# Masked attention layer on one core: the start laid anew, later tokens turned by VectorE squares and DMA

## What is computed

```python
h = jnp.maximum(_layernorm(x, axis=-1), 0.0)
q = (h @ Wq + bq).reshape(b, n, H, HD)
k = (h @ Wk + bk).reshape(b, n, H, HD)
v = (h @ Wv + bv).reshape(b, n, H, HD)
scores = jnp.einsum('bqhd,bkhd->bhqk', q, k) / jnp.sqrt(jnp.float32(HD))
scores = scores + (1.0 - adj)[None, None, :, :] * -1000000000.0
attn = jax.nn.softmax(scores, axis=-1)
out = jnp.einsum('bhqk,bkhd->bqhd', attn, v).reshape(b, n, d)
x = x + out @ Wo + bo
```

## Time and profile before

| | us |
|---|---|
| Median of 3 runs (1120.91 to 1122.2) | 1121.8 |
| The profiled execution | 1119.4 |
| Its span, first to last instruction | 1117.6 |
| PE busy, share of the span | 1096.1, 98% |
| ACT busy | 997.8, 89% |
| DVE busy | 958.5, 86% |
| POOL busy | 315.4, 28% |
| Mean busy share of the DMA engines, by tenths of the span | 0.1 to 0.8, highest in the first twentieth |
| TensorE clock granted, mean | 0.997 of full |

### The profile page before, as it was taken

One profiled execution on the slowest core, in us unless ns is written; L12 is line 12 of the kernel. 1 busy time (PEld: TensorE's weight loads), 2 busy tenths in 40 slices (PEclk: granted clock), 3 DMA queues, 4 the chain that ended last, 5 costly groups with the idle time before them and its releaser, 6 DMA issues.

```text
span 1117.6 us, 28309 instructions
## 1 busy us (share of the span) xinstructions
PE 1096.1 (98%) x10672; PEld 886.7 (79%) x10672; DVE 958.5 (86%) x1796; ACT 997.8 (89%) x1835; POOL 315.4 (28%) x508
## 2 busy tenths in 40 slices
PE   8799999999999999999999999999999999999997
PEld 6677887888878888887887887888877888878775
DVE  5698988988989888998989988998988988988885
ACT  3699999998989998999999999999999999999985
POOL 6364212232214222242212412124112242112122
PEclk9899999999999999999999999999999999999999
DMA  7842352424424243332424335242352424424111
GB/s 202 253 109 50 88 147 64 105 61 111 135 72 104 64 126 101 86 102 69 130 77 116 76 81 142 68 118 75 82 141 73 103 68 101 106 65 105 51 29 49
DMA packets 88374, 109.08 MB, mean 98 GB/s; under 512 B 24752, under 2 KB 50480, under 8 KB 88240
## 3 DMA queue, kind: packets, MB, share of 16 engines
q1 hardware_dynamic: 77040, 95.89, 31.6%
q0 software_dynamic: 11008, 11.13, 5.1%
q10 hardware_dynamic: 192, 0.26, 0.1%
HBM read 30.54 MB, written 9.44 MB: 36 GB/s over the span
## 4 chain that ended last, share of the span: by engine, by line
issue 51%; DMA 30%; POOL 15%; SPq 1%; PE 1%; DVE 0%; POOLq 0%; ACT 0%; ACTq 0%; DVEq 0%
DMA inv_rows<-inv_turned 15%; DMA inv_t<-inv_rows 14%; POOL inv_t L446 10%; POOL xn L414 3%; POOL ln_t L399 1%; POOL mask L453 1%; SPq L298 1%; PE ps_scores L752 0%; POOL ln_neg_mean L396 0%; DMA q_stack<-q_lo 0%; PE ps_heads L782 0%; PE ps_side L800 0%; POOL ln_var L397 0%; POOL ln_t L403 0%; POOL ln_t L401 0%
## 5 line engine op out<-in xcount | busy, mean ns | idle before, releaser
L567 DVE CUSTOM_DVE_ANT_0 rows<-ps_scores,mask 128x1024 f32<-128x1024 f32 x512 | 615.7, 1217 | 36.4 <-PE ps_scores L733 31.1
L478 ACT ACTIVATE rows<-rows,row_min 128x1024 f32<-128x1024 f32 x512 | 589.5, 1158 | 3.6 <-DVE row_min L567 3.6
L766 PE MATMUL ps_turn<-ident_r,rows_raw 128*128 128x128 f32 x4096 | 465.6, 258 | 11.6 <-ACT turned_a L483 10.6
L766 PEld LDWEIGHTS ps_turn<-ident_r,rows_raw 128*128 128x128 f32 x4096 | 400.4, 141 | 87.0 <-ACT rows L478 29.0
L483 ACT ACTIVATE turned_a<-ps_turn 128x512 f32<-128x512 f32 x512 | 307.7, 601 | 87.1 <-PE ps_turn L766 87.0
L733 PE MATMUL ps_scores<-k_stack,q_stack 128*128 128x512 f32 x1016 | 328.7, 423 | 0.9 <-DVE row_min L567 0.9
L574 DVE COPY turned_b<-ps_turn 128x512 f32<-128x512 f32 x312 | 215.0, 689 | 85.9 <-PE ps_turn L766 80.7
L440 POOL DMA_DIRECT2D inv_rows<-inv_turned x64 | 46.6, 727 | 622.0 <-DVE inv_turned L608 616.6
L446 POOL DMA_DIRECT2D inv_t<-inv_rows x256 | 136.0, 538 | 149.1 <-DMA inv_rows<-inv_turned 144.8
L733 PEld LDWEIGHTS ps_scores<-k_stack,q_stack 128*128 128x128 f32 x1016 | 159.5, 188 | 16.9 <-DVE row_min L567 6.2
L817 PE MATMUL ps_heads<-turned_a,v 128*32 128x256 f32 x2048 | 123.8, 382 | 0.3 <-ACT turned_a L483 0.3
(11 more groups left out here) (84 smaller groups left out, 588.8 us busy)
## 6 DMA issues: line engine op xcount, KB each, us to landing
q_stack<-q_hi SPq DMA_DIRECT2D x248, 64.0 KB, 2.0
q_stack<-q_lo SPq DMA_DIRECT2D x248, 64.0 KB, 2.0
k_stack<-k_hi SPq DMA_DIRECT2D x242, 64.0 KB, 2.0
k_stack<-k_lo SPq DMA_DIRECT2D x242, 64.0 KB, 2.0
res<-in_x SPq DMA_DIRECT2D x32, 256.0 KB, 2.8
inv_t<-inv_rows POOLq DMA_DIRECT2D x256, 32.0 KB, 2.3
out<-res SPq DMA_DIRECT2D x32, 256.0 KB, 2.8
xn<-in_x SPq DMA_DIRECT2D x30, 256.0 KB, 3.2
```

The source lines that it names most:

```text
L478: nc.scalar.activation(rows[:, k, :], rows[:, k, :], ACT.Exp, bias=row_min[:, k:k + 1], scale=-1.0, accum_out=row_sum[:, u % 2, j:j + 1]). ...
L567: nc.vector.tensor_tensor_reduce(out=rows[:, k, :], in0=ps_scores[n % 2][:], in1=mask[:, qt, :], scale=1.0, scalar=START_MIN, op0=ALU.add, ...
L766: tr = nc.tensor.transpose(ps_turn[half][:, k, :].bitcast(F32R), rows_raw[:, n % RING, kt * P:(kt + 1) * P], ident_r[:])
```

## The change

1. **Tokens of batches 1 to 7.** The ht steps on PE and ACT are gone. `xn` now holds tokens as `(p t)`, so that a partition has eight neighbouring tokens. POOL norms in two halves and in two passes a tile (subtract and cut at zero, then scale). DVE turns 64 features of all tiles in one instruction, four for a batch; POOL writes each block of 32 features to DRAM (8 DMAs of 128 KB), and SP reads `ht` back (4 DMAs of 256 KB: half 0 at the end of phase 0, half 1 at the start of phase 1). Moments move to phase 1 of the batch before, `load_x` waits for the squares and not for PE.
2. **Inverse sums.** Two broadcast DMAs a unit for four; `INV_ROW` 6 to 7, `NORM_ROW` 2 to 3.
3. **Schedule tables.** Ahead counts and places changed, 33 second-bank copies of a batch's 64 on ACT (25 before); "v" 0 first in phase 1 and "o" 3 before "v" 1 in phase 0; the reload of `res` is issued later.
4. **Start.** Weights q and k on ACT's queue, o and its biases on POOL's; the root of the first deviations on ACT (with a table load of its own) and the rest on DVE; the scores of rows 0 and 1 in two halves of the keys ("keys"), the first before the last qk steps; five banks for the qk steps; the v steps moved behind the first slot.
5. **First unit.** `FIRST_STEPS` gives v at rows 1 to 6 and the qk steps from row 9; ahead counts 4, 3, 2 in it. SP stacks a head of step 0, a head each of steps 1 and 3, then the other heads of step 1; the tokens of batch 1 are loaded before step 2 is stacked and the 2 MB of masks after it. Masks of tiles 4 to 7 are put in final form by DVE at slots 9, 12, 17 and 21.

The diff, cut to its core:

```diff
-INV_ROW, NORM_ROW = 6, 2
+INV_ROW, NORM_ROW = 7, 3
-HT_ROWS = {(0, 29): 0, (0, 30): 1, (1, 4): 2, (1, 6): 3}
+FIRST_STEPS = (("first_v", 0, (1, 2, 3, 3)), ("first_v", 1, (4, 5, 6, 6)), ("qk", 0, (9, 10, 11, 11)),
+               ("qk", 1, (13, 13, 14, 14)), ("qk", 2, (17, 18, 19, 19)), ("qk", 3, (21, 21, 22, 22)),
+               ("v", 0, (25, 26, 27, 27)), ("v", 1, (28, 29, 30, 30)))
+FIRST_SCORES, FIRST_MASKS, FIRST_EXPS = 4, 3, 2
-START_STEPS = (("ht", 0), ("ht", 1), ("qk", 0), ("qk", 1), ("ht", 2), ("ht", 3), ("bo", 0), ("qk", 3), ("qk", 2),
-               ("rows", 0), ("v", 0), ("rows", 2), ("v", 1))
+START_STEPS = (("ht", 0), ("ht", 1), ("qk", 0), ("qk", 1), ("ht", 2), ("ht", 3), ("bo", 0), ("qk", 3), ("keys", 0),
+               ("keys", 1), ("qk", 2), ("rows", 2))
+SQUARE_ROWS, FIRST_SQUARE_ROWS = (17, 17, 22, 24), (24, 25, 26, 28)
+MASK_ROWS = (9, 12, 17, 21)
...
             sp.wait_ge(lo_done, START_QK.index(3) + 1)
-            stack_step(sp, 0, 3, start_stacked, range(PARTS - SP_HEADS, PARTS))
+            stack_step(sp, 0, 3, start_stacked, range(SP_K_HEADS))
+            stack_step(sp, 0, 1, start_stacked, range(SP_K_HEADS, PARTS), high=start_hi, low=start_lo)
 
             sp.wait_ge(scores_done, PARTS)
-            load_mask(2, MASKS_EARLY, MASKS_LATE)
+            load_mask(MASKS_EARLY, MASKS_EARLY, MASKS_LATE)
+            for piece in range(X_PIECES):
+                load_x(1, piece)
             sp.wait_ge(lo_done, START_QK.index(2) + 1)
             stack_step(sp, 0, 2, stacked["q"][0])
-            load_mask(3, MASKS_LATE, TILES)
-            for piece in range(X_PIECES):
-                load_x(1, piece)
+            load_mask(MASKS_EARLY + 1, MASKS_LATE, TILES)
...
+            def ht_back(b, c):
+                cols = slice(c * BANK, (c + 1) * BANK)
+                for n in range(SQUARE_RING):
+                    uses = (b * SQUARES - 1 - n) // SQUARE_RING + 1
+                    sp.wait_ge(squares_out[n], uses * PAIR * 16)
+                sp.wait_ge(qk_done, qk_step(b - 1, 1, c * CHUNKS + 1) + 1)
+                sp.wait_ge(v_done, v_step(b - 1, 1, c) + 1)
+                for k in range(DCH):
+                    sp.dma_start(ht[:, k, cols], tokens_t[k * P:(k + 1) * P, cols]).then_inc(ht_in[c], 16)
...
+            def put_squares(b, pair):
+                n = (b - 1) * SQUARES + pair
+                pool.wait_ge(squares_done, n + 1)
+                for j in range(PAIR):
+                    block = pair * PAIR + j
+                    pool.dma_start(tokens_t[block * SQUARE:(block + 1) * SQUARE, :].rearrange("i (c n) -> c i n", c=PARTS),
+                                   squares[:, n % SQUARE_RING, j, :]).then_inc(squares_out[n % SQUARE_RING], 16)
...
-                for h in range(PARTS):
-                    pool.dma_start(inv_t[h * HEAD_DIM:(h + 1) * HEAD_DIM, :, :],
-                                   by_head[h].partition_broadcast(HEAD_DIM)
-                                   ).then_inc(inv_in, 16)
+                for t in range(UNIT_TILES):
+                    pool.dma_start(inv_t[:, t, :], inv_rows[t * PARTS:(t + 1) * PARTS, :].unsqueeze(1).to_broadcast(
+                        [PARTS, HEAD_DIM, P])).then_inc(inv_in, 16)
...
+            def first_root(half):
+                act.wait_ge(moments_done, (half + 1) * PARTS)
+                nc.scalar.activation(ln["t0"][:, tiles], mean_var[:, tiles, 1], ACT.Abs_reciprocal_sqrt, bias=eps_col[:]
+                                     ).then_inc(first_roots, 1)
...
+            def turn_squares(b, pair):
+                n, at = (b - 1) * SQUARES + pair, pair * PAIR * SQUARE
+                dve.wait_ge(normed, (b + 1) * TILES)
+                nc.vector.transpose(squares[:, n % SQUARE_RING].rearrange("p c (j t) -> p t c j", t=TILES),
+                                    xn[:, :, at:at + PAIR * SQUARE].rearrange("p t (c i) -> p t c i", i=SQUARE)
+                                    ).then_inc(squares_done, 1)
...
+                for t in range(MASKS_LATE, TILES):
+                    if first and MASK_ROWS[t - MASKS_LATE] == i:
+                        dve.wait_ge(mask_in[MASKS_EARLY + 1], 16)
+                        nc.vector.tensor_scalar(mask[:, t, :], mask[:, t, :], 1.0, -MASKED, ALU.subtract, ALU.mult
+                                                ).then_inc(mask_late_ready, 1)
...
-                        pe.wait_ge(ht_done, (b + 1) * HT_STEPS + (c + 1) * DCH)
+                        pe.wait_ge(ht_in[c], (b + 1) * DCH * 16)
```

More of the change, by code:

```diff
@@ L100, in steps @@
         return LAST_STEPS
-    return [(kind, s, at) for kind, s, at in STEPS[g] if not (first and g == 0 and kind == "o")]
+    return FIRST_STEPS if first and g == 0 else STEPS[g]
 def side_work(g, i, first, last):
@@ L248, in unit, with reach @@
             return b * BATCH_UNITS + (g * UNITS + u)
-        def reach(ahead, n):
-            return range(n + ahead[(n - 1) % UNIT_ROWS], min(n + ahead[n % UNIT_ROWS] + 1, BATCH * BATCH_ROWS))
+        def reach(ahead, first_ahead, n):
+            before, here = (first_ahead if m < UNIT_ROWS - 1 else ahead[m % UNIT_ROWS] for m in (n - 1, n))
+            return range(n + before, min(n + here + 1, BATCH * BATCH_ROWS))
         def step_ended(b, g, i):
@@ L634, in _ @@
             nc.vector.memset(row_inv[:], 0.0).then_inc(inv_zeroed, 1)
+            nc.vector.memset(eps_col[:], EPS).then_inc(eps_ready, 1)
             dve.sem_inc(copied_b, START)
[L636 to L641 removed]
@@ L659, in _ @@
-            copy_v(0, 0, 0, V_BANKS[0])
-            for n in range(2, MASK_AHEAD[-1]):
+            for half in range(2):
+                tiles = slice(half * PARTS, (half + 1) * PARTS)
+                for t in range(half * PARTS, (half + 1) * PARTS):
+                    moments(0, t)
+                first_deviations(half, tiles)
+                for t in range(half * PARTS, (half + 1) * PARTS):
+                    nc.vector.tensor_scalar(xn[:, t, :], xn[:, t, :], ln["neg_mean"][:, t:t + 1],
+                                            ln["rstd"][:, t:t + 1], ALU.add, ALU.mult).then_inc(normed, 1)
@@ L661, in _ @@
+            first_low_part(0)
+            first_mask(0)
+            first_mask(1)
+            dve.wait_ge(o_weights_in, 3 * 16)
+            dve.wait_ge(bo_done, 1)
+            nc.vector.tensor_tensor(bo_row[:], BO_BANK, bo_row[:], ALU.add).then_inc(bo_ready, 1)
+            first_low_part(1)
+            first_low_part(2)
+            for n in range(2):
                 mask_row(n)
-            copy_v(0, 0, 1, V_BANKS[1])
+            first_low_part(3)
+            first_mask(2)
+            for n in range(2, FIRST_MASKS):
+                mask_row(n)
@@ L861, in slot @@
                 turn(b, g, i, 1)
-                if row(b, g, i) == 0:
-                    for m in range(PARTS, SCORES_AHEAD[-1]):
-                        scores(m)
-                for m in reach(SCORES_AHEAD, row(b, g, i)):
+                for m in reach(SCORES_AHEAD, FIRST_SCORES, row(b, g, i)):
                     scores(m)
@@ L869, in slot @@
                         heads(unit(b, g, u) - 1, u + 1, g if u else 1 - g, half)
-                if (g, i) in HT_ROWS and not last:
-                    s = HT_ROWS[g, i]
-                    pe.wait_ge(normed, (b + 1) * TILES + (s // DCH + 1) * PARTS)
-                    pe.wait_ge(heads_normed, unit(b, g, u))
-                    pe.wait_ge(ht_done, (b + 1) * HT_STEPS + s)
-                    for t in range(PIECES):
-                        turn_ht(s, t)
                 kind, s, pieces = side_work(g, i, first, last)
@@ L888, in slot @@
                         values(1 - g, s, piece)
+                    elif kind == "first_v":
+                        values(0, s, piece)
                     else:
```

345 lines of the change are left out of this document (210 added, 135 removed), and 6 rows, old and new, of the table STEPS.

## The result

The changed kernel takes **1186.2 us** (median of 4 runs, 1182.9 to 1188.6) where the kernel before takes 1122.0 beside it: a ratio of 1.0571, 95% interval 1.0551 to 1.0592. The forecast was 1103.8 and its range 1095 to 1113; the change went the other way, by 64 us. The profiled execution took 1182.9 us with a span of 1181.1.

A forecast was written before the change was run, and what follows sets the result against it. PE was taken as the bound from the second unit on, at 16.6 us a unit. Terms -9.9 + 1.2 - 12.8 + 4 - 0.5 = -18.0 gave 1101.4, plus 2.4 for the median 1103.8 us; 8-in-10 range 1095 to 1113.

The forecast's parts named there:

- Tokens off PE, -9.9: Seven batches: PE loses the ht steps' extra time in two units of each batch, -9.9 us if ACT and DVE follow.
- SP gets four issues ... a wait of some us there costs nothing: SP's queue in phase 1: stacks behind the ht reads are first due at row 9, so waiting costs 0.
- (d): Rival: ht comes late from DRAM by as much as PE saved, 2.5 us a batch; about 1121 us, chance 0.03.
- Squares, 0.7 us: DVE's four 128x512 squares a batch: 0.7 us each, near the 128x512 copy; upper price 3.4 us each.
- rival (c): DVE's squares make the kernel slower; gain used up at 3.8 us a set, 1139 us at 5; chance 0.08.
- stay under half busy: POOL, with eight more tile passes and eight DMA issues but 16 fewer broadcast issues a batch, stays under half busy.
- The other units of phase 0, -0.5: Batch 0: the other three units of phase 0 take 49.8 us in all, against 50.3 before: -0.5 us.
- The late masks, +4: First phase: DVE waits for the 2 MB of masks till about 51.5 us, PE behind it: +4 us (0 to 7).
- The start and first unit, -12.8: Start to first heads: first masking at 20.5, first turn at 25.0, first heads at 40.9 against 53.66 us: -12.8 us.
- my own bound of 27: Sign at the start: the prediction is wrong if the first turn comes later than 27 us.
- The end, +1.2: Last unit: the inverse starts some 2.2 us later, less 1.1 for two fewer issues: +1.2 us (0 to 2).
- Of tables ... nothing: Schedule tables: number of pieces and of changes between kinds of products on PE stays the same, so no effect.

The follow-up runs named there:

- e6: e1 with steps qk 3 and v 0 of phase 0 exchanged (qk 3 at row 17 in place of 21): 1132.0 us, ratio 1.0081.
- e12: e6 with POOL's two norming passes made of other operations (add-and-multiply, then cut-off): 1132.6 us, ratio 1.0093.
- e1: The changed kernel with the next tokens' loads issued at step 1 of phase 1 in place of step 2: 1137.4 us, ratio 1.0138.
- e2: The changed kernel with phase 1's side steps in the order of before (qk 0, qk 1, v 0, qk 2): 1146.8 us, ratio 1.0229.
- e10: e9 with the first phase's qk steps at rows 7, 10, 14, 18 and batch 1's tokens and moments moved: 1125.9 us, ratio 1.0027.
- e5: e1 with the 2 MB of late masks issued ahead of the tokens and of step 2's stack: 1133.4 us, ratio 1.0111.
- e4: The changed kernel with the root's activation table loaded early, ahead of ACT's wait for the moments: 1185.5 us, ratio 1.0574.
- e11: e10 with SP holding the v weights and first masks back till batch 0's tokens have landed: 1123.4 us, ratio 1.0013.
- e7: e1 with the rows of the inverse and its use put back (INV_ROW 6, NORM_ROW 2): 1153.4 us, ratio 1.0284.
- e9: e1 with masks first, k stack sooner, table early, and the inverse a row sooner in the last unit alone: 1127.6 us, ratio 1.0051.
- e13: e6 with the six tables of order inside the eight rows and the inverse's rows as before the change: 1177.1 us, ratio 1.0498.

## Why the prediction was wrong, step by step

**Tokens off PE, -9.9.** The gain on PE itself was right: six of eight units came to 16.5 to 16.7, and with the queues mended the two units that had held the ht steps take 9.5 (e6) and 9.8 us (e12) less over the seven batches, where I had 9.9. The other six units together lose 4.1 and 3.2 us of it, most in the last unit of phase 1, which takes 16.6 to 18.0 in both; so the stretch as a whole gives -5.4 and -6.6. As built the term was **+47.0**. The step that failed is "SP gets four issues ... a wait of some us there costs nothing": it followed SP's queue to the first stack behind the four issues and no further. I had the price in hand, 9.8 us for 16 stack DMAs, and used it at the start only. In phase 1 the third such step comes 6.5 us behind the second, so the queue is 4.8 us late there, and the token loads, now due 16 rows sooner, were never given a due time; that the moments had moved I read in the diff and did not price. It is shown by e1 and e2, from two sides, 44.4 us of waiting against 3.8 and 12.1, and 47.0 us over the kernel before against 0.0 and 7.3 in the stretch. No rival held this: (d) had the right kind of cause, a late transfer, at the wrong transfer. The transfer I watched, `ht` back from DRAM, had its cover: it lands in 4.3 us (the median), not 3.2, and in the list of PE's waits it does not occur.

**Squares, 0.7 us.** They took 1.18:

```profile
L720 DVE STREAM_TRANSPOSE squares<-xn 128x512 f32<-128x512 f32 x5 | 5.7, 1184 | 0.0
```

The Trainium skill's figure (VectorE: DVE Perf Modes, "The three transpose paths"), from which I had estimated 1.24, was the better guide than the copy's row, although it is for bf16. The time did not depend on it, as argued: the point from which rival (c) decides was 3.8.

**POOL.** It was to stay under half busy, and did (310 of 988 us), but its two passes take 1143 and 920 ns a tile where one of 556 did it before; I had counted eight more passes and no price. Nothing waited for them.

**The other units of phase 0, -0.5.** From the first heads to slot 32 the change takes 117.12 - 48.97 = 68.2 us, not 53.8 (49.8 and 4 for the masks). This is the second failed step: I put these 24 slots at the old 50.3 although four "qk" steps now stand in them. 9.25 us are the wait at 108.39, the same queue again, in its mirror form: idle for 15.6 us, then 48 us of issues. Some 4 are the late masks. The waits do not add up, as e10 shows: with both gone, the 24 slots still take 109.90 - 46.33 = 63.6 us, at a granted clock of 1.00, and in them

```profile
DVE q_lo L677 <- ACT q_hi L571: 8.2, 2, 4.1
...
ACT q_hi L571 <- PE ps_side L927: 7.2, 2, 4.0
ACT turned_a L561 <- PE ps_turn L920: 6.1, 5, 2.1
PE ps_turn L920 <- ACT turned_a L561: 5.5, 7, 1.4
```

stand in e10's waits. The kernel before has, between its first heads and slot 32, 0.2 us for DVE's `q_lo`, 1.2 for PE's `turned_a` and 3.0 for ACT's. Four "qk" steps instead of two, the late masks' final form and the squares came into this stretch; PE is busy in it for 53.3 us in e10 and 48.5 in the kernel before. That this crowding is the cause of the rest is argued from those waits and not shown; no run takes only it away.

**The late masks, +4.** Near: 4.5 in the unit by e5, 4.0 in the time, where the intervals overlap. DVE waited till 56.93, not 51.5.

**The start and first unit, -12.8.** The first heads came at 48.97, not at 40.9: the term was -4.7. Norming at 9.30 where 7.2 was said: the table load that I had hidden in a wait stood in the path (1.28, e4), and the tokens landed later, the first moments at 4.29 us (3.54 in the kernel before), the second half of the tokens in 8.1 us against 5.3, with the weights on three queues beside them (that these are the reason is not shown: with the v weights and masks held back, in e11, it was 8.1 again). Masking at 24.51 (20.5), first turn at 29.09 (25.0), past my own bound of 27; then 19.9 us to the heads for 15.9 said, at a clock of 0.67 between 30 and 40 us. That is a mean of the two levels: 0.50 (1.2 GHz) from 30 to 36 us, 1.00 (2.4 GHz) from 38 on; PE had waited 0.74 us ahead of 27.04 and 0.64 us ahead of 30.60, both times for DVE:

```profile
core 0: us, PE busy (x) PEld busy (x) DVE busy (x) ACT busy (x) POOL busy (x), PEclk, DMA share, GB/s
...
30.00:40.00 10.00, 9.40 (x58) 8.57 (x58) 8.17 (x15) 7.87 (x15) 2.24 (x2) 0.67 0.69 201
```

This part is also chance: e1 has the same start, its clock stood at 1.00 over those 10 us, and its first heads came at 45.45; e12's came at 49.34. Even 45.45 misses 40.9 by 4.5 us. And what a sooner start is worth was itself misjudged: e4's first heads came 3.7 us sooner (45.29), and slot 32 no sooner (117.26).

**The end, +1.2.** It was +3.4 and, with the rest mended, +4.5 in e6. The last inverse starts 1.7 us ahead of the last heads, where it was 3.5 before, and DVE waits 7.1 us for it (2.94 before):

```profile
1174.82 0.42 DVE L738 TENSOR_TENSOR heads_t<-ps_heads,inv_t 128x256 f32<-128x256 f32 x1 [7.14 <-DMA inv_t<-inv_rows]
...
1175.38 2.45 PE L952 MATMUL ps_side<-wo,heads_t 128*128 128x256 f32 x8 [3.35 <-DVE heads_t L738]
```

The two issues of 686 ns land in 3.0 us, the four of 538 ns before in 2.3, so fewer of them saved nothing. Behind PE's wait of 3.35 us its last products took 2.45 us for 1.97, at a granted clock of 0.78 (3.61 in e6 behind 3.23 us; but 1.97 again in e1 behind 3.46, at a clock of 1.00, so such a wait does not always cost this). My step priced the row (a slot and a copy, less the issues). Moving the row back alone gives nothing: in e7 and e9 the inverse then stands at the last exponential and starts 1.8 us ahead of the heads. With the six tables back as well, in e13, it starts 3.4 us ahead and the end is as before. So the row and the order around it hold it together; which table, most simply how far the exponentials lead, is not shown.

**"Of tables ... nothing."** Wrong: the tables are worth a great deal, though only beside the new steps. e7 put back the rows of the inverse and lost 16 us; e13 put back these and the six tables, and lost 47 in the seven batches (982.3 against 935.3). That this equals the +47.0 above is chance.

## What to carry to other kernels

When a step is moved, write out every issuing queue past the new place, with the price of an issue and the row at which each consumer asks; a queue that is idle on the average can be overbooked for a few steps, and what is late can be what stands behind the steps that moved. A sooner start is worth only what the next fixed wait leaves of it. And hand-laid tables that changed along with the steps are part of the change's worth: in e7 and e13 putting one half back alone lost 16 and 47 us.
